# Second batch's product with x in three fp32r products of 512 columns, turned back through DRAM

## The chip, the cores and the metric

One core of one Trainium2 chip. The time is that of the whole program on the device, in microseconds (us), the median of the runs shown. Engines: PE (TensorE) multiplies, DVE (VectorE), ACT (ScalarE) and POOL (GpSimd) do the rest, SP (SyncE) issues most DMAs.

## What is computed

x is (8, 512, 128): 8 batches of 512 tokens, in float32. Per batch:

```
xn  = layernorm(layernorm(x)) * gamma + beta
q, k, v = split(xn @ w_qkv); k = softmax over the tokens
attn = (k^T v per head) applied to q * 32**-0.5, @ w_out + b_out
x1  = x + layernorm(attn + y)                 y = layernorm(x)
x1n = layernorm(x1)
ffn = sum over 8 experts of (silu(x1n @ Wg) * (x1n @ Wu)) @ Wd     Wg, Wu (128, 512), Wd (512, 128)
out = x1 + layernorm(ffn)
```

## The kernel before

The feed-forward part is the bulk of it. Each batch has 32 steps (STEPS: 8 experts times 4 blocks of 128 hidden columns), and a body of the program is one batch, b from 0 to 7. A step s does three 512-column products into a gate bank, three into an up bank and, for the step three before it (LAG), three into the accumulator `acc_ps`. Three products stand for one float32 product: operands are split into fp32r parts `_hi` and `_lo`, and `products` (L1248) adds hi*hi, hi*lo and lo*hi. ACT takes silu of the gate bank (L777), DVE multiplies it with the up bank (L1050), ACT copies the result to `h_hi` (L752) and DVE subtracts to get `h_lo` (L1037). Up to step 29 of the first batch (H_IN_PSUM) h is written back into the up bank, of which there are three. So the up product of step s + 3 waits, in `gate_up` (L1255), for `h_lo` of step s (`s_read`, `s_hlo`).

Between these steps the attention part of the next batch is done in small pieces. Which piece runs at which step on which engine is written in tables: FIRST_PE, FIRST_DVE, FIRST_ACT and FIRST_POOL for body 0 (which does the second batch's attention), PE_AT and so on for the others. Every engine runs its own list in order. On ACT and DVE a piece named in FRONT stands ahead of the step's own work, others behind it; on PE a piece stands behind the step's nine products; on POOL pieces stand ahead of the weight blocks of LO_AT. In body 0 the weights are still being loaded and split: SP loads block m into one of six raw buffers, once POOL has made the lo part of block m - 6 (`load_w`, L461 to L472), ACT makes the hi part (HI_AT), POOL the lo part (`split_lo`, L395), block m one step after ACT. Block m is matrix m % 3 (gate, up, down) of expert m // 3; its products start at step 4 * (m // 3).

The attention of a batch is folded. With E = exp(k - max) it makes A from E and the normalised x (piece A), M by the heads (piece M: eight small matmuls in `through_heads`, L1280, for the second batch; two full products with a mask for later ones), G = wq M (piece G), then x times G into `att_ps` (piece attn). For batches from the third on x times G is done with G as the stationary operand, in three fp32r products of 512 columns. That gives the result transposed, so it is turned back: DVE transposes 32x32 blocks into `t_blk["z"]` (piece z_T, L957), SP stores them to a DRAM tensor and loads them in four pieces into `t_out["z"]` (`store_blocks`, `load_blocks`, L496 to L503), and DVE adds `yb` to get z (L965). `t_blk["z"]` is the same buffer as `t_blk["E"]`, and `t_out["z"]` the same as `zn`. For the second batch (body 0, `first`) the product has x as the stationary operand: four float32 products of 128 columns (L1321), which leave tokens on the partitions, and z is one addition out of PSUM (L962). Behind z come its statistics (z_stats), POOL's rstd, zn and x1, DVE's x1_stats, POOL's x1n and again a turn through DRAM (x1n_T) for the next body's gate and up products.

Of the kernel before, what the change touches and what calls it, by code (L numbers as in the profile page):

```python
# [33 lines left out]
FIRST_DVE = {"E_T": 4, "next_stats": 8, "A": 12, "M": 13, "z": 15, "z_stats": 16, "next_T": 18, "wk_lo": 20,  # L34
             "x1_stats": 20, "x1n_T": 24, "next_xnT_lo": 28, "x1n_lo": 31}
FIRST_ACT = {"E_store": 5, "E_load": 8, "G": 14, "wk_hi": 18, "next_xnT": 26, "next_xnT_hi": 27, "x1n_hi": 30}
FIRST_POOL = {"y": 2, "yb": 6, "next_rstd": 10, "next_xn": 13, "z_rstd": 17, "x1": 17, "x1_rstd": 21}
# [47 lines left out]
def build(nc, x, gamma, beta, w_qkv, w_out, b_out, Wg, Wu, Wd, out):  # L85
# [10 lines left out]
    with ctx:  # L96
# [120 lines left out]
        att_v = att_ps[:, :].rearrange("p (j d) -> p j d", j=J)  # L217
# [241 lines left out]
        def _(sp):  # L459
# [26 lines left out]
            for m in range(6, NW):  # L486
                load_w(m)
                if m == 8:
                    sp.wait_ge(s_f_x1ps, J)
                    load_x(2, 0)  # L490

# [8 lines left out]
            def load_blocks(k, n):  # L500
                sp.wait_ge(s_t_store[k], n * 16)
                for dst, src in exchange(k):
                    sp.dma_start(dst, src).then_inc(s_t_load[k], 16)  # L503

            def body(b, par, first, nxt, last):
                if nxt and not first:
                    sp.wait_ge(s_x1, b)
                    load_x(b + 2, par)
                if not first:
                    if not last:  # L510
                        store_blocks("E", s_E_blk, b + 1)
                    store_blocks("acc", s_acc, b)
                    if not last:
                        load_blocks("E", b + 1)
                    load_blocks("acc", b)

                if not first and not last:
                    store_blocks("z", s_z_blk, b)

                    sp.wait_ge(s_x1, b)  # L520
                    load_blocks("z", b)
# [169 lines left out]
        def _(act):  # L691
# [5 lines left out]
            def attention(at, c, par, first):  # L697
# [188 lines left out]
        def _(dve):  # L886
# [24 lines left out]
            def attention(at, c, par, first):  # L911
# [10 lines left out]
                if at == "wk_lo":  # L922
                    dve.wait_ge(s_wk_hi, 1)
                    dve.tensor_tensor(wk_lo[:, :], wqkv[:, D:2 * D], wk_hi[:, :].bitcast(F32),
                                      ALU.subtract).then_inc(s_wk_lo, 1)
                if at == "next_xnT_lo":
                    dve.wait_ge(s_xnT_hi, c - 1)
                    dve.tensor_tensor(xnT_lo[:, :], xnT[:, :], xnT_hi[:, :].bitcast(F32),
                                      ALU.subtract).then_inc(s_xnT_lo, 1)
# [28 lines left out]
                if at == "z":  # L958
                    dve.wait_ge(s_yb, c)
                    if first:  # L960
                        dve.wait_ge(s_attn_ps, c)
                        dve.tensor_tensor(z[:, :, :], att_v, yb[:, :, :], ALU.add).then_inc(s_z, 1)  # L962
                    else:
                        dve.wait_ge(s_t_load["z"], (c - 1) * 64)
                        dve.tensor_tensor(z[:, :, :].rearrange("p j (i r) -> p j i r", r=32), from_group(t_out["z"][:, :]),  # L965
                                          yb[:, :, :].rearrange("p j (i r) -> p j i r", r=32), ALU.add).then_inc(s_z, 1)
# [12 lines left out]
                if at == "E_T":  # L979
                    dve.wait_ge(s_ET, c)  # L980
                    if c > 2:

                        dve.wait_ge(s_t_store["z"], (c - 2) * 16)
# [263 lines left out]
        def _(pe):  # L1247
# [39 lines left out]
            def attention(at, c, first):  # L1287
                if at == "kT":
                    pe.wait_ge(s_xnT_hi, c - 1)
                    products(att_ps[:, :], wk_hi[:, :], wk_lo[:, :], pairs(xnT_hi[:, :]), pairs(xnT_lo[:, :]), True, True,  # L1290
                             s_xnT_lo, c - 1).then_inc(s_kT_ps, 1)
# [20 lines left out]
                if at == "attn" and not first:  # L1312

                    pe.wait_ge(s_G, c)
                    pe.wait_ge(s_G_lo, c - 1)
                    products(att_ps[:, :], G_hi[:, :], G_lo[:, :], pairs(xnT_hi[:, :]), pairs(xnT_lo[:, :]), True, True,
                             s_xnT_lo, c - 1).then_inc(s_attn_ps, 1)
                elif at == "attn":
                    pe.wait_ge(s_G, c)
                    for j in range(J):  # L1320
                        last = pe.matmul(att_ps[:, j * D:j * D + D], xnT[:, j * P:j * P + P], G_sb[:, :],  # L1321
                                         start=True, stop=True)
                    last.then_inc(s_attn_ps, 1)
# [272 lines left out]
```

## Time and profile before

| | |
|---|---|
| median of 3 runs | 542.60 us (542.57 to 542.65) |
| the profiled execution's own time | 542.58 us |
| its span, first to last instruction | 540.7 us |
| mean granted TensorE clock | 0.999 of full speed |
| busy share of the span | PE 99%, weight loads 86%, DVE 82%, ACT 64%, POOL 31% |
| DMA traffic | 28.68 MB, mean 53 GB/s |

The time of a run is a little more than the span, since it holds what lies around the program. Times in the rows are us from the span's start. Matmuls are pipelined: a record's length is longer than the distance to the next start, so the pace of PE is read from start times. Some instructions of a float32 product appear as two records.

### The profile page before, as it was taken

To read this page: it belongs to the slowest core of one execution; us is meant where nothing else is said; L and a number is where in the kernel's file an instruction comes from. 1 tells how busy PE (TensorE), PEld (TensorE's weight loads), DVE (VectorE), ACT (ScalarE), POOL (GpSimd) and SP (SyncE) were. 2 spreads that over 40 slices of the span, in tenths; PEclk is the share of its full clock that TensorE was granted. 3 is DMA by queue.
4 is the path that set the end of the run, shared out by engine and by line. 5 is a ranking of instruction groups with operands and counts; after the bars stand their busy time and mean duration, and the time that the engine had idled before them with its cause. 6 is when DMAs were issued, how large, how long until landed. Compare 5 with 4: busy or idle time off the path is not lost.

```text
span 540.7 us, 8660 instructions
## 1 busy us (share of the span) xinstructions
PE 534.3 (99%) x2584; PEld 466.2 (86%) x2584; DVE 442.5 (82%) x967; ACT 348.4 (64%) x633; POOL 169.0 (31%) x221
## 2 busy tenths in 40 slices
PE   8999999999999999999999999999999999999997
PEld 6788888888888888888888888888888888888886
DVE  7896877899777997879977898688987799777866
ACT  5986877557674565855667566665767555655555
POOL 6796950217102280114602045021540016000101
PEclk9999999999999999999999999999999999999999
DMA  6354111120220201202102112021111110110000
GB/s 199 108 168 116 41 59 50 30 78 21 60 73 7 96 23 39 79 19 79 52 8 79 40 59 59 0 79 39 60 39 44 35 61 0 41 39 1 20 2 19
DMA packets 33797, 28.68 MB, mean 53 GB/s; under 512 B 3411, under 2 KB 25686, under 8 KB 33750
## 3 DMA queue, kind: packets, MB, share of 16 engines
q1 hardware_dynamic: 32736, 27.47, 16.2%
q10 hardware_dynamic: 1014, 0.66, 0.4%
q8 instruction: 20, 0.33, 0.3%
q14 instruction: 27, 0.22, 0.1%
HBM read 17.37 MB, written 10.75 MB: 52 GB/s over the span
## 4 chain that ended last, share of the span: by engine, by line
PE 98%; ACT 1%; DVE 1%; DMA 0%; issue 0%; POOL 0%; DVEq 0%; POOLq 0%; SPq 0%
PE acc_att_ps L1251 11%; PE acc_att_ps L1250 11%; PE acc_att_ps L1253 11%; PE gate_ps L1250 10%; PE gate_ps L1251 10%; PE up_ps L1251 10%; PE up_ps L1250 10%; PE gate_ps L1253 10%; PE up_ps L1253 10%; PE acc_att_ps L1296 1%; DMA x_in<-in_L_attn_x_dram 0%; ACT xh L843 0%; PE acc_att_ps L1311 0%; PE acc_att_ps L1308 0%; PE acc_att_ps L1302 0%
## 5 line engine op out<-in xcount | busy, mean ns | idle before, releaser
L777 ACT ACTIVATE gs<-gate_ps 128x512 f32<-128x512 f32 x255 | 152.2, 597 | 171.3 <-PE gate_ps L1253 170.3
L1050 DVE TENSOR_TENSOR h<-gs,up_ps 128x512 f32<-128x512 f32 x231 | 157.5, 682 | 75.8 <-PE up_ps L1253 65.9
L1037 DVE TENSOR_TENSOR h_lo<-h,h_hi 128x512 fp32r<-128x512 f32 x230 | 171.5, 745 | 0.0
L752 ACT ACTIVATE h_hi<-h 128x512 fp32r<-128x512 f32 x230 | 143.5, 624 | 6.5 <-DVE h L1050 5.1
L1250 PE MATMUL gate_ps<-x1nT_hi,wg_hi 128*128 128x512 f32 (+1 forms) x254 | 98.4, 387 | 0.0
L1251 PE MATMUL gate_ps<-x1nT_hi,wg_lo 128*128 128x512 f32 (+1 forms) x254 | 96.1, 378 | 0.0
L1253 PE MATMUL gate_ps<-x1nT_lo,wg_hi 128*128 128x512 f32 (+1 forms) x254 | 96.1, 378 | 0.0
L1250 PE MATMUL up_ps<-x1nT_hi,wu_hi 128*128 128x512 f32 (+1 forms) x254 | 96.1, 378 | 0.0
L1251 PE MATMUL up_ps<-x1nT_hi,wu_lo 128*128 128x512 f32 (+1 forms) x254 | 96.1, 378 | 0.0
L1253 PE MATMUL up_ps<-x1nT_lo,wu_hi 128*128 128x512 f32 (+1 forms) x254 | 96.1, 378 | 0.0
L1250 PE MATMUL acc_att_ps<-h_hi,wd_hi 128*128 128x512 f32 x252 | 95.5, 379 | 0.0
L1251 PE MATMUL acc_att_ps<-h_hi,wd_lo 128*128 128x512 f32 x252 | 95.5, 379 | 0.0
L1253 PE MATMUL acc_att_ps<-h_lo,wd_hi 128*128 128x512 f32 x252 | 95.5, 379 | 0.0
L550 POOL TENSOR_TENSOR rstd_fin<-mv_fin,expo 128x4 f32<-128x4 f32 (+2 forms) x10 | 8.8, 888 | 172.2 <-DVE mv_fin L890 140.0
L1253 PEld LDWEIGHTS up_ps<-x1nT_lo,wu_hi 128*128 128x128 f32 x254 | 48.0, 189 | 6.8
L1253 PEld LDWEIGHTS acc_att_ps<-h_lo,wd_hi 128*128 128x128 f32 x252 | 47.6, 189 | 7.2
L1253 PEld LDWEIGHTS gate_ps<-x1nT_lo,wg_hi 128*128 128x128 f32 x254 | 48.0, 189 | 6.8
L1251 PEld LDWEIGHTS up_ps<-x1nT_hi,wu_lo 128*128 128x128 f32 x254 | 48.0, 189 | 6.8
L1250 PEld LDWEIGHTS up_ps<-x1nT_hi,wu_hi 128*128 128x128 f32 x254 | 48.0, 189 | 6.8
L1251 PEld LDWEIGHTS acc_att_ps<-h_hi,wd_lo 128*128 128x128 f32 x252 | 47.6, 189 | 6.7
L1250 PEld LDWEIGHTS acc_att_ps<-h_hi,wd_hi 128*128 128x128 f32 x252 | 47.6, 189 | 6.7
L1251 PEld LDWEIGHTS gate_ps<-x1nT_hi,wg_lo 128*128 128x128 f32 x254 | 48.1, 189 | 6.0
(296 smaller groups left out, 565.0 us busy)
## 6 DMA issues: line engine op xcount, KB each, us to landing
w_raw<-in_L_ffn_Wg_dram SPq DMA_DIRECT2D x8, 256.0 KB, 3.0
w_raw<-in_L_ffn_Wu_dram SPq DMA_DIRECT2D x8, 256.0 KB, 2.9
w_raw<-in_L_ffn_Wd_dram SPq DMA_DIRECT2D x8, 256.0 KB, 2.9
x_in<-in_L_attn_x_dram SPq DMA_DIRECT2D x7, 256.0 KB, 2.9
t_dram_x1n<-t_blk_x1n SPq DMA_DIRECT2D x7, 256.0 KB, 2.0
t_out_x1n<-t_dram_x1n SPq DMA_DIRECT2D x28, 64.0 KB, 1.9
t_dram_acc<-t_blk_acc SPq DMA_DIRECT2D x7, 256.0 KB, 2.3
t_out_acc<-t_dram_acc SPq DMA_DIRECT2D x28, 64.0 KB, 2.0
```

The lines of the kernel that those rows point to most:

```text
L550: pool.tensor_tensor(rstd[k][:, 0, toks], mv[k][:, toks, 1], expo[:, toks], ALU.pow).then_inc(done, 1)
L752: act.activation(h_hi[s % NH][:, :], h_of(t, s)[:, :], ACT.Copy).then_inc(s_hhi, 1)
L777: act.activation(gs[q][:, :], gate_ps[q][:, :], ACT.Silu).then_inc(s_silu, 1)
L1037: dve.tensor_tensor(h_lo[s % NH][:, :], h_of(t, s)[:, :], h_hi[s % NH][:, :].bitcast(F32), ALU.subtract).then_inc(s_hlo, 1)
L1050: dve.tensor_tensor(h_of(t, s)[:, :], gs[q][:, :], up_ps[q][:, :], ALU.mult).then_inc(s_h, 1)
L1250: pe.matmul(ps, w_h, x_h, start=start, stop=False)
L1251: pe.matmul(ps, w_l, x_h, start=False, stop=False)
L1253: return pe.matmul(ps, w_h, x_l, start=False, stop=stop)
L1296: last = pe.matmul(att_ps[:, 0:D].rearrange("p (i r) -> p i r", r=32), xh[:, j, :], from_group(t_out["E"][:, :])[:, j], start=(j == 0), st ...
```

## The change

The second batch's x times G takes the form that the later batches have. PE does three fp32r products of 512 columns. ACT makes G_hi for it as for the others, DVE makes G_lo at step 14. Its x is split too: ACT makes `xnT_hi` at step 10 (own_xnT_hi) and DVE `xnT_lo` at step 11 (own_xnT_lo). Since this batch's `xnT` has its columns in another order, the two write through a view that puts them in the order of the other batches, with a step of two elements. The result is turned back: z_T at step 15, SP's store and four loads, z at step 18 instead of 15, z_stats at 18 instead of 16, next_T at 17 instead of 18, x1_stats at 21 instead of 20. On POOL z_rstd and x1 move from step 17 to 20, x1_rstd from 21 to 22. SP does the store and the loads ahead of the last weight block's load. M for this batch stays with the products through the heads. The counts that later batches wait for go up by one.

```diff
-FIRST_DVE = {"E_T": 4, "next_stats": 8, "A": 12, "M": 13, "z": 15, "z_stats": 16, "next_T": 18, "wk_lo": 20,
-             "x1_stats": 20, "x1n_T": 24, "next_xnT_lo": 28, "x1n_lo": 31}
-FIRST_ACT = {"E_store": 5, "E_load": 8, "G": 14, "wk_hi": 18, "next_xnT": 26, "next_xnT_hi": 27, "x1n_hi": 30}
-FIRST_POOL = {"y": 2, "yb": 6, "next_rstd": 10, "next_xn": 13, "z_rstd": 17, "x1": 17, "x1_rstd": 21}
+FIRST_DVE = {"E_T": 4, "next_stats": 8, "own_xnT_lo": 11, "A": 12, "M": 13, "G": 14, "z_T": 15, "next_T": 17,
+             "z": 18, "z_stats": 18, "wk_lo": 20, "x1_stats": 21, "x1n_T": 24, "next_xnT_lo": 28, "x1n_lo": 31}
+FIRST_ACT = {"E_store": 5, "E_load": 8, "own_xnT_hi": 10, "G": 14, "wk_hi": 18, "next_xnT": 26, "next_xnT_hi": 27,
+             "x1n_hi": 30}
+FIRST_POOL = {"y": 2, "yb": 6, "next_rstd": 10, "next_xn": 13, "z_rstd": 20, "x1": 20, "x1_rstd": 22}
...
+        def in_two_by_two(v):
+            return v.rearrange("p (h l q) -> p h l q", h=JH, l=JH)
+
+        def pairs_of_two_by_two(v):
+            return v.rearrange("p (l q h) -> p h l q", h=JH, l=JH)
...
-            for m in range(6, NW):
+            for m in range(6, NW - 1):
                 load_w(m)
                 if m == 8:
                     sp.wait_ge(s_f_x1ps, J)
                     load_x(2, 0)
...
+            store_blocks("z", s_z_blk, 1)
+            load_blocks("z", 1)
+            load_w(NW - 1)
...
+                if at == "own_xnT_hi":
+                    act.wait_ge(s_xnT, 1)
+                    act.activation(pairs_of_two_by_two(xnT_hi[:, :]), in_two_by_two(xnT[:, :]),
+                                   ACT.Copy).then_inc(s_xnT_hi, 1)
...
+                if at == "own_xnT_lo":
+                    dve.wait_ge(s_xnT_hi, 1)
+                    dve.tensor_tensor(pairs_of_two_by_two(xnT_lo[:, :]), in_two_by_two(xnT[:, :]),
+                                      pairs_of_two_by_two(xnT_hi[:, :]).bitcast(F32), ALU.subtract).then_inc(s_xnT_lo, 1)
...
                 if at == "z":
                     dve.wait_ge(s_yb, c)
-                    if first:
-                        dve.wait_ge(s_attn_ps, c)
-                        dve.tensor_tensor(z[:, :, :], att_v, yb[:, :, :], ALU.add).then_inc(s_z, 1)
-                    else:
-                        dve.wait_ge(s_t_load["z"], (c - 1) * 64)
-                        dve.tensor_tensor(z[:, :, :].rearrange("p j (i r) -> p j i r", r=32), from_group(t_out["z"][:, :]),
-                                          yb[:, :, :].rearrange("p j (i r) -> p j i r", r=32), ALU.add).then_inc(s_z, 1)
+                    dve.wait_ge(s_t_load["z"], c * 64)
+                    dve.tensor_tensor(z[:, :, :].rearrange("p j (i r) -> p j i r", r=32), from_group(t_out["z"][:, :]),
+                                      yb[:, :, :].rearrange("p j (i r) -> p j i r", r=32), ALU.add).then_inc(s_z, 1)
...
-                if at == "attn" and not first:
+                if at == "attn":
 
                     pe.wait_ge(s_G, c)
-                    pe.wait_ge(s_G_lo, c - 1)
+                    pe.wait_ge(s_G_lo, c)
                     products(att_ps[:, :], G_hi[:, :], G_lo[:, :], pairs(xnT_hi[:, :]), pairs(xnT_lo[:, :]), True, True,
-                             s_xnT_lo, c - 1).then_inc(s_attn_ps, 1)
-                elif at == "attn":
-                    pe.wait_ge(s_G, c)
-                    for j in range(J):
-                        last = pe.matmul(att_ps[:, j * D:j * D + D], xnT[:, j * P:j * P + P], G_sb[:, :],
-                                         start=True, stop=True)
-                    last.then_inc(s_attn_ps, 1)
+                             s_xnT_lo, c).then_inc(s_attn_ps, 1)
```

What the tables do to the order is seen at three places. The first is DVE at steps 11 to 13 of body 0, between the step's own pairs of `up_ps` (h, in the up bank) and `h_lo`. Before:

```order
L935 RECIPROCAL erec<-esum 128x1
L939 COPY A_sb<-acc_att_ps 128x128
L1050 TENSOR_TENSOR up_ps<-gs,up_ps 128x512
L1037 TENSOR_TENSOR h_lo<-up_ps,h_hi 128x512
L948 SCALAR_TENSOR_TENSOR M_sb<-acc_att_ps,erec,R_sb 128x128
```

Now:

```order
L942 TENSOR_TENSOR xnT_lo<-xnT,xnT_hi 128x2x256
L953 RECIPROCAL erec<-esum 128x1
L957 COPY A_sb<-acc_att_ps 128x128
L1064 TENSOR_TENSOR up_ps<-gs,up_ps 128x512
L1051 TENSOR_TENSOR h_lo<-up_ps,h_hi 128x512
L966 SCALAR_TENSOR_TENSOR M_sb<-acc_att_ps,erec,R_sb 128x128
```

xnT_lo stands ahead of erec and A_sb, for which PE's products through the heads wait.

The second is DVE from z on, steps 15 to 18. Before:

```order
L962 TENSOR_TENSOR z<-acc_att_ps,yb 128x512
L1050 TENSOR_TENSOR up_ps<-gs,up_ps 128x512
L1037 TENSOR_TENSOR h_lo<-up_ps,h_hi 128x512
L1050 TENSOR_TENSOR up_ps<-gs,up_ps 128x512
L1037 TENSOR_TENSOR h_lo<-up_ps,h_hi 128x512
L904 BN_STATS st_z<-z 128x6 x4
L890 BN_AGGR mv_z<-st_z 128x2 x4
L900 TENSOR_SCALAR nm_z<-mv_z 128x4
L1050 TENSOR_TENSOR up_ps<-gs,up_ps 128x512
L1037 TENSOR_TENSOR h_lo<-up_ps,h_hi 128x512
L1050 TENSOR_TENSOR up_ps<-gs,up_ps 128x512
L1037 TENSOR_TENSOR h_lo<-up_ps,h_hi 128x512
```

Now:

```order
L975 STREAM_TRANSPOSE t_blk_E<-acc_att_ps 128x512
L1064 TENSOR_TENSOR up_ps<-gs,up_ps 128x512
L1051 TENSOR_TENSOR h_lo<-up_ps,h_hi 128x512
L1064 TENSOR_TENSOR up_ps<-gs,up_ps 128x512
L1051 TENSOR_TENSOR h_lo<-up_ps,h_hi 128x512
L1064 TENSOR_TENSOR up_ps<-gs,up_ps 128x512
L1051 TENSOR_TENSOR h_lo<-up_ps,h_hi 128x512
L991 STREAM_TRANSPOSE t_blk_x<-xh 128x512
L979 TENSOR_TENSOR z<-zn,yb 128x512
L1064 TENSOR_TENSOR up_ps<-gs,up_ps 128x512
L1051 TENSOR_TENSOR h_lo<-up_ps,h_hi 128x512
L918 BN_STATS st_z<-z 128x6 x4
```

A transpose into t_blk_E (the shared block buffer) has z's place; z comes three steps later, behind next_T's transpose of x, and ahead of step 18's h; its statistics follow h and h_lo.

The third is SP and POOL. SP before, and now:

```order
L472 DMA w_raw<-in_L_ffn_Wu_dram 128x512
L472 DMA w_raw<-in_L_ffn_Wd_dram 128x4x128
L498 DMA t_dram_x<-t_blk_x 128x512
L503 DMA t_out_x<-t_dram_x 32x4x128 x4
```

```order
L478 DMA w_raw<-in_L_ffn_Wu_dram 128x512
L498 DMA t_dram_z<-t_blk_E 128x512
L503 DMA zn<-t_dram_z 32x4x128 x4
L478 DMA w_raw<-in_L_ffn_Wd_dram 128x4x128
L498 DMA t_dram_x<-t_blk_x 128x512
L503 DMA t_out_x<-t_dram_x 32x4x128 x4
```

POOL before, and now:

```order
L395 TENSOR_TENSOR wd_lo<-w_raw,wd_hi 128x512
L550 TENSOR_TENSOR rstd_z<-mv_z,expo 128x4
L565 TENSOR_SCALAR zn<-z,nm_z,rstd_z 128x128 x4
L598 TENSOR_TENSOR x_1<-zn,x_in 128x512
L395 TENSOR_TENSOR wg_lo<-w_raw,wg_hi 128x512
L395 TENSOR_TENSOR wu_lo<-w_raw,wu_hi 128x512
L395 TENSOR_TENSOR wd_lo<-w_raw,wd_hi 128x512
```

```order
L395 TENSOR_TENSOR wd_lo<-w_raw,wd_hi 128x512
L395 TENSOR_TENSOR wg_lo<-w_raw,wg_hi 128x512
L395 TENSOR_TENSOR wu_lo<-w_raw,wu_hi 128x512
L560 TENSOR_TENSOR rstd_z<-mv_z,expo 128x4
L575 TENSOR_SCALAR zn<-z,nm_z,rstd_z 128x128 x4
L608 TENSOR_TENSOR x_1<-zn,x_in 128x512
L395 TENSOR_TENSOR wd_lo<-w_raw,wd_hi 128x512
```

On SP the turn of z stands between the loads of blocks 22 and 23. On POOL the lo parts of blocks 18 and 19 have moved ahead of rstd_z, zn and x1.

## Rows read from the trace of the kernel before

**Rows 1.** The page's head: span, then busy time of each engine.
```profile
span 540.7 us, 8660 instructions
...
PE 534.3 (99%) x2584; PEld 466.2 (86%) x2584; DVE 442.5 (82%) x967; ACT 348.4 (64%) x633; POOL 169.0 (31%) x221
```

**Rows 2.** The chain that ended last, share of the span by engine.
```profile
PE 98%; ACT 1%; DVE 1%; DMA 0%; issue 0%; POOL 0%; DVEq 0%; POOLq 0%; SPq 0%
```

**Rows 3.** What PE waited for: us in total, times, longest.
```profile
PE up_ps L1407 <- DVE warm L1075: 1.0, 1, 1.0
PE gate_ps L1533 <- ACT x1nT_hi L860: 0.6, 1, 0.6
```

**Rows 4.** PE's timeline in body 0: start, us, engine, line, operation, out<-in, count.
```profile
42.82 0.43 PE L1284 MATMUL acc_att_ps<-U_sb,A_sb 128*32 128x128 f32 x8
...
47.39 1.05 PE L1321 MATMUL acc_att_ps<-G_sb,xnT 128*128 128x128 f32 x8
48.20 0.46 PE L1250 MATMUL gate_ps<-x1nT_hi,wg_hi 128*128 128x512 f32 x1
48.50 0.38 PE L1251 MATMUL gate_ps<-x1nT_hi,wg_lo 128*128 128x512 f32 x1
...
60.59 0.38 PE L1250 MATMUL up_ps<-x1nT_hi,wu_hi 128*128 128x512 f32 x1
```

**Rows 5.** PE's timeline in body 1, the third batch's product with x.
```profile
108.77 0.38 PE L1250 MATMUL acc_att_ps<-xnT_hi,G_hi 128*128 128x512 f32 x1
...
109.42 0.38 PE L1250 MATMUL gate_ps<-x1nT_hi,wg_hi 128*128 128x512 f32 x1
109.63 0.38 PE L1251 MATMUL gate_ps<-x1nT_hi,wg_lo 128*128 128x512 f32 x1
```

**Rows 6.** DVE's timeline in body 0.
```profile
31.90 1.17 DVE L1037 TENSOR_TENSOR h_lo<-h,h_hi 128x512 fp32r<-128x512 f32 x1
...
40.98 0.29 DVE L939 COPY A_sb<-acc_att_ps 128x128 f32<-128x128 f32 x1
...
51.76 0.70 DVE L1050 TENSOR_TENSOR up_ps<-gs,up_ps 128x512 f32<-128x512 f32 x1 [0.65 <-PE up_ps L1253]
...
52.96 0.86 DVE L904 BATCH_NORM_STATS2 st_z<-z 128x6 f32<-128x128 f32 x4
...
54.48 0.70 DVE L1050 TENSOR_TENSOR up_ps<-gs,up_ps 128x512 f32<-128x512 f32 x1
...
56.88 0.70 DVE L977 STREAM_TRANSPOSE t_blk_x<-xh 128x512 f32<-128x512 f32 x1
```

**Rows 7.** POOL's timeline in body 0.
```profile
30.78 1.73 POOL L592 TENSOR_TENSOR yb<-y,bout_bc 128x512 f32<-128x512 f32 x1
...
40.47 1.27 POOL L395 TENSOR_TENSOR wg_lo<-w_raw,wg_hi 128x512 fp32r<-128x512 f32 x1
...
54.34 1.01 POOL L550 TENSOR_TENSOR rstd_z<-mv_z,expo 128x4 f32<-128x4 f32 x1 [2.26 <-DVE mv_z L890]
...
58.52 1.28 POOL L395 TENSOR_TENSOR wg_lo<-w_raw,wg_hi 128x512 fp32r<-128x512 f32 x1
```

**Rows 8.** DMA issues in SP's timeline: start, time of issuing, queue, line, out<-in, count.
```profile
49.28 0.33 SPq L472 DMA_DIRECT2D w_raw<-in_L_ffn_Wu_dram  x1
...
112.46 2.85 SPq L503 DMA_DIRECT2D zn<-t_dram_z  x4
...
175.38 0.34 SPq L498 DMA_DIRECT2D t_dram_z<-t_blk_E  x1
177.45 1.73 SPq L503 DMA_DIRECT2D zn<-t_dram_z  x4
...
435.45 0.34 SPq L498 DMA_DIRECT2D t_dram_z<-t_blk_E  x1
438.71 1.77 SPq L503 DMA_DIRECT2D zn<-t_dram_z  x4
```

**Rows 9.** DMA issues by kind: count, KB each, median us from issue to landing.
```profile
zn<-t_dram_z SPq DMA_DIRECT2D x24, 64.0 KB, 1.9
```

More of the change, by code:

```diff
@@ L216, in build @@
         att_ps = two_ps[:, 512:1024]
-        att_v = att_ps[:, :].rearrange("p (j d) -> p j d", j=J)
         z_ps = [ps[:, 0:D] for ps in (gate_ps[1], up_ps[1], gate_ps[2], acc_ps)]
@@ L485, in _ @@
             sp.dma_start(bout_bc[:, :], b_out.rearrange("(a d) -> a d", a=1).to_broadcast([P, D])).then_inc(s_bout, 16)
-            for m in range(6, NW):
[L487 to L490, printed above, removed]
             def store(c):
@@ L503, in load_blocks @@
                     sp.dma_start(dst, src).then_inc(s_t_load[k], 16)
+            for m in range(6, NW - 1):
+                load_w(m)
+                if m == 8:
+                    sp.wait_ge(s_f_x1ps, J)
+                    load_x(2, 0)
+            store_blocks("z", s_z_blk, 1)
+            load_blocks("z", 1)
+            load_w(NW - 1)
             def body(b, par, first, nxt, last):
@@ L517, in body @@
                 if not first and not last:
-                    store_blocks("z", s_z_blk, b)
+                    store_blocks("z", s_z_blk, b + 1)
                     sp.wait_ge(s_x1, b)
-                    load_blocks("z", b)
+                    load_blocks("z", b + 1)
                 if nxt:
@@ L731, in attention @@
                     act.wait_ge(s_G_ps, c)
-                    act.activation(G_sb[:, :] if first else G_hi[:, :], att_ps[:, 0:D], ACT.Copy).then_inc(s_G, 1)
+                    act.activation(G_hi[:, :], att_ps[:, 0:D], ACT.Copy).then_inc(s_G, 1)
                 if at == "x1n_hi":
@@ L925, in attention @@
                                       ALU.subtract).then_inc(s_wk_lo, 1)
+                if at == "own_xnT_lo":
+                    dve.wait_ge(s_xnT_hi, 1)
+                    dve.tensor_tensor(pairs_of_two_by_two(xnT_lo[:, :]), in_two_by_two(xnT[:, :]),
+                                      pairs_of_two_by_two(xnT_hi[:, :]).bitcast(F32), ALU.subtract).then_inc(s_xnT_lo, 1)
                 if at == "next_xnT_lo":
-                    dve.wait_ge(s_xnT_hi, c - 1)
+                    dve.wait_ge(s_xnT_hi, c)
                     dve.tensor_tensor(xnT_lo[:, :], xnT[:, :], xnT_hi[:, :].bitcast(F32),
@@ L980, in attention @@
                     dve.wait_ge(s_ET, c)
-                    if c > 2:
-                        dve.wait_ge(s_t_store["z"], (c - 2) * 16)
+                    if c > 1:
+                        dve.wait_ge(s_t_store["z"], (c - 1) * 16)
                     dve.transpose(grouped(t_blk["E"][:, :]), by_group(ET[:, :])).then_inc(s_E_blk, 1)
@@ L1288, in attention @@
                 if at == "kT":
-                    pe.wait_ge(s_xnT_hi, c - 1)
+                    pe.wait_ge(s_xnT_hi, c)
                     products(att_ps[:, :], wk_hi[:, :], wk_lo[:, :], pairs(xnT_hi[:, :]), pairs(xnT_lo[:, :]), True, True,
-                             s_xnT_lo, c - 1).then_inc(s_kT_ps, 1)
+                             s_xnT_lo, c).then_inc(s_kT_ps, 1)
                 if at == "A":
```

## The prediction

> **What bounds the kernel now.** I read the page's head first: PE is busy in 99% of a span of 540.7 us [rows 1]. Busy time alone doesn't make a bound, so the chain that ended last comes next: 98% of it is PE [rows 2]. The list of what PE waited for settles it: five waits, 2.5 us in sum, all of one occurrence, and the last in time is that on x1nT_hi ahead of the very first gate product (L1533); the longest two stand in [rows 3]. From there on PE never waits. So two things count: PE time added or removed behind that goes into the span one to one, and work on any other engine costs nothing until a product stands waiting for it. A 512-column product starts 0.21 to 0.22 us after the one before it [rows 5]; a step of nine takes 1.94 us.
>
> **The edit on PE.** Before, the four 128-column float32 products L1321 run as eight records from 47.39 us, the next gate product starts at 48.20 and the one behind it at 48.50 [rows 4]: 1.11 us from the first record to the gate's second product. In the third batch the same place already has three fp32r products of 512 columns: 108.77 to 109.42, and 109.63 for the gate's second product, 0.86 us [rows 5]. The difference, 0.25 us, contains both the products and the slower start of the gate product behind them. It is the only PE work that changes: **-0.25 us**, and everything on PE behind step 14 comes that much earlier. Eight records for four products say that float32 takes more than one pass. The Trainium skill (TensorE: Matmul & The Clock Gate, section "Wait — 56ns, not 53.3ns?") gives 55.6 ns start to start for 128 columns at the high clock and 215.7 ns for 512; by that alone the old form would be 0.44 us, the new one 0.65, and the edit would cost 0.20 us instead of gaining 0.25.
>
> **The split of xnT.** ACT's copy to xnT_hi stands behind h_hi at step 10. ACT is busy in 64% of the span [rows 1], so one more copy, even one stretched to over 1 us by its 8-byte step, is caught up within a step or two. Price 0. The DVE subtraction xnT_lo comes behind h_lo at step 11 and ahead of erec and A_sb (40.98 us before), on which PE's products through the heads wait. It reads two SBUF tiles, and POOL runs wg_lo from 40.47 for 1.27 us, so POOL is there first [rows 6, 7]. At 31.90 such a subtraction took 1.17 us instead of 0.68: it ended 0.56 us behind the end of POOL's yb [rows 6, 7]. So xnT_lo ends about 42.3, and A_sb (0.29 us [rows 6]) about 42.6 where it ended at 41.3; PE's products start at 42.82 [rows 4]. Price 0, with 0.1 to 0.2 us to spare. Bounds: nothing, and 1.1 us if POOL's next operation (1.3 us) goes ahead as well; I take 0, since at 31.90 DVE got its turn behind one POOL operation. G_lo reads 128 columns as A_sb does, 0.3 us, behind G_hi on ACT; G's products are a step of 1.94 us ahead of those that need it at 47.39, and DVE waits for PE in each of these steps: 0.
>
> **The way back through DRAM.** Before, z was one addition out of PSUM, done right behind the product. Now: a transpose (0.70 us, as [rows 6] show for t_blk_x) that ends near 49.0; the store by SP; four loads; z at step 18. SP reaches the store behind load_w of block 22, which waits for POOL's wu_lo and went out at 49.28 [rows 8]. So the store goes out about 49.65. In a typical later batch the first load follows 2.07 us behind the store (175.38, 177.45), the four are issued in 1.73 us [rows 8] and each lands 1.9 us after its issue [rows 9]: last landing 49.65 + 2.07 + 1.30 + 1.9 = **54.9 us**. In the last batch the first load came 3.26 us behind the store (435.45, 438.71) and in the third batch the four issues took 2.85 us [rows 8]: these late ones put the landing at 56.1, both together (with loads that then land later) at about 57.3.
>
> DVE itself gets to z no earlier: without z's statistics at step 16, step 17's h goes out when PE is ready for it, 53.45 (step 16's was at 51.76 [rows 6]; a step of 1.94 later, 0.25 earlier), then h_lo and t_blk_x, so z is reached at 55.35. There it meets POOL again, because wg_lo of block 18, held behind zn and x1 before (58.52, [rows 7]), now runs as soon as ACT has made wg_hi, which ACT does at the end of step 17: an estimate of 54.4 to 55.65, 0.95 us behind that step's h and 1.27 long. By the 31.90 row DVE is free about 0.5 us behind that end: h of step 18 at 56.15. Then h_lo of 17 (57.35), the statistics (1.52 us, 52.96 to 54.48 [rows 6]), h of 19 at 58.87, h_lo of 18 done at 60.15. Who waits for that: PE's up product of step 21 overwrites the PSUM bank h_lo reads; it started at 60.59 [rows 4], now 60.34. **Margin 0.2 us**, price 0.
>
> The second limit: rstd_z starts 1.38 us behind the start of z's statistics (52.96, 54.34) and x1 is ready 4.18 us later (58.52) [rows 6, 7]: now 58.73 and 62.9, perhaps 63.2 with wk_lo colliding with zn. DVE's x1 statistics at step 21 therefore start at 63.2, h of 22 at 64.7, h_lo of 21 is done at 66.0; the up product of step 24 wants it at 66.17. Again 0.2 us. Behind that all is loose: x1n is ready about 67.4, DVE turns it at 68.3 anyway; POOL's three last lo blocks end near 71, PE wants them from 73.3; load_w of block 23 goes out behind the z loads, near 53.8, and ACT converts it at step 23, over 10 us later; t_blk_x's store goes out earlier than before.
>
> **Sum.** 542.58 (the profiled execution, span 540.7 and what lies around it) - 0.25 + 0 = 542.33. The median of the runs shown is 542.60, 0.02 above; I predict **542.35 us**. A measurement of this kernel tells from no change about 0.2%, 1.1 us; my forecast is inside it.
>
> **Rivals.**
> 1. The z round trip is late and PE pays. Each 0.1 us that the data land behind about 55.7 us comes off the 0.2 us margin and then stalls PE as much. One late piece (56.1): stall 0.4 to 0.6, total 542.7. For it: load_w's 256 KB go ahead of the store on the same queue, and the tightest margins are 0.2 us, while my landing times are good to 0.5. Against: four of six later round trips took the typical time and leave 0.7 us.
> 2. The same place, both pieces late (57.0 and more): DVE stands at z, behind it h of 18, h_lo of 17 and 18, and PE at step 21 for 1.4 us or more: 543.7 to 544.0, slower by over 0.2%. It decides from a landing at 57.0 on. For it: each of the two delays shows in one of the six round trips of the trace. Against: never both in one.
> 3. PE waits at the products through the heads. If POOL's wu_lo goes ahead of xnT_lo too, A_sb is ready near 43.8 and PE loses 1.0 us: 543.3. The order in which DVE and POOL take turns decides. In the rows DVE waited for one operation only. The Trainium skill (SBUF — State Buffer, section "SBUF: two separate sides") has it that whichever of the two starts first holds the shared port pair for its whole instruction and the other is blocked fully; the 1.17 us row agrees for one instruction, and the page doesn't say who is next.
> 4. The new products are not cheaper. If the old form cost only what 128-column products cost at one pass each, the time is about 542.8. The start times of 47.39 and 48.20 speak against it, since PE is full on both sides. The page's rates above would bring this.
> 5. It does more than its 0.25 us on PE: nothing in the list of PE's waits is left to remove, so faster by over 1.1 us has no mechanism here.
>
> **How the numbers follow.** Forecast 0.62 (542.2 to 542.5); rival 1 0.22 (542.5 to 543.2); rival 2 0.06; rival 3 0.06 (543.0 to 543.6); rival 4 0.02; rival 5 0.02. The range 542.2 to 543.2 holds the forecast, rival 1 and part of rivals 3 and 4, 0.87 in all, and leaves out little more than rival 2. Within 0.2% are the forecast, rivals 1 and 4 and nearly all of 3: 0.91; slower 0.07; faster 0.02.
>
> **What would show it.** Right: three records of acc_att_ps from xnT_hi and xnT_lo at 47.4 us, 0.65 us to the gate product; the list of PE's waits with the same five rows; xnT_lo lasting about 1.5 us with A_sb ending before 42.8; z starting near 55.4 and lasting 0.8 us; h_lo of step 18 done before 60.3. Wrong: a new row in PE's waits on h_lo (rivals 1, 2) or on A_sb (rival 3), or DVE idle ahead of z until a DMA. A time below 541.5 would mean that the old products cost more than their start times say.

## The result and the profile after

| | before | after |
|---|---|---|
| median | 542.60 us (542.49 to 542.81, 5 runs) | 544.55 us (544.42 to 544.62, 5 runs) |
| span of the profiled execution | 540.7 us | 542.8 us |
| mean granted TensorE clock | 0.999 | 0.999 |
| ratio after / before | | 1.0035, 95% interval 1.0024 to 1.0046 |

The change costs 1.9 to 2.1 us. The forecast of 542.35 and its range up to 543.2 are both missed, on the side of rival 2. Runs of one kernel spread by about 0.7 us (the kernel before in a later series: 542.39 to 543.12), so amounts below that are read from start times within the traces.

The page's head of the kernel after, beside [rows 1]; PE's busy time is longer by 0.8 us only, so most of the 2.1 us must be idle time.

```profile
span 542.8 us, 8662 instructions
...
PE 535.1 (99%) x2579; PEld 466.1 (86%) x2579; DVE 445.5 (82%) x970; ACT 349.0 (64%) x634; POOL 169.5 (31%) x221
```

What PE waited for, the first three rows. Beside [rows 3] there is one new row, and it is now the largest: up products that wait for `h_lo`.

```profile
PE up_ps L1264 <- DVE h_lo L1051: 1.5, 2, 1.0
PE up_ps L1415 <- DVE warm L1089: 1.0, 1, 1.0
PE gate_ps L1541 <- ACT x1nT_hi L874: 0.6, 1, 0.6
```

PE's timeline, beside [rows 4, 5]: the new product at 47.46, the two waits, and the third batch's product, the place of [rows 5].

```profile
47.46 0.38 PE L1264 MATMUL acc_att_ps<-xnT_hi,G_hi 128*128 128x512 f32 x1
...
48.10 0.38 PE L1264 MATMUL gate_ps<-x1nT_hi,wg_hi 128*128 128x512 f32 x1
48.32 0.38 PE L1265 MATMUL gate_ps<-x1nT_hi,wg_lo 128*128 128x512 f32 x1
...
58.25 0.38 PE L1267 MATMUL gate_ps<-x1nT_lo,wg_hi 128*128 128x512 f32 x1
59.63 0.45 PE L1264 MATMUL up_ps<-x1nT_hi,wu_hi 128*128 128x512 f32 x1 [1.00 <-DVE h_lo L1051]
59.92 0.38 PE L1265 MATMUL up_ps<-x1nT_hi,wu_lo 128*128 128x512 f32 x1
...
61.43 0.38 PE L1267 MATMUL gate_ps<-x1nT_lo,wg_hi 128*128 128x512 f32 x1
62.26 0.48 PE L1264 MATMUL up_ps<-x1nT_hi,wu_hi 128*128 128x512 f32 x1 [0.45 <-DVE h_lo L1051]
62.58 0.38 PE L1265 MATMUL up_ps<-x1nT_hi,wu_lo 128*128 128x512 f32 x1
...
110.55 0.38 PE L1264 MATMUL acc_att_ps<-xnT_hi,G_hi 128*128 128x512 f32 x1
```

From 47.46 to 48.32 are 0.86 us where 1.11 stood: the product gains its 0.25 us. Then the up product of step 20 starts 1.38 us behind the gate product instead of 0.22 (1.16 lost), and the one behind it 0.29 later instead of 0.22 (0.07). At step 21 it is 0.83 (0.61 lost) and 0.32 (0.10). In sum 1.94 us are lost at two instructions. Body 0 also ran 0.07 us later from the start (42.89 for the products through the heads, which did not wait, against 42.82). 1.94 + 0.07 - 0.25 = 1.76, and at the third batch's product the kernel is 110.55 - 108.77 = 1.78 us late. The rest, 0.3 us, comes at 290 us, in body 4, where the change touches nothing:

```profile
290.01 0.38 PE L1265 MATMUL acc_att_ps<-h_hi,wd_lo 128*128 128x512 f32 x1
290.42 0.48 PE L1267 MATMUL acc_att_ps<-h_lo,wd_hi 128*128 128x512 f32 x1
290.74 0.38 PE L1264 MATMUL gate_ps<-x1nT_hi,wg_hi 128*128 128x512 f32 x1
```

0.41 and 0.32 us stand where 0.22 and 0.22 are usual. The list of waits doesn't count this gap.

Why `h_lo` is late stands in the timelines of SP, DVE and POOL of body 0, to be read beside [rows 8], [rows 6] and [rows 7].

```profile
49.34 0.33 SPq L478 DMA_DIRECT2D w_raw<-in_L_ffn_Wu_dram  x1
49.71 0.43 SPq L498 DMA_DIRECT2D t_dram_z<-t_blk_E  x1
53.27 1.75 SPq L503 DMA_DIRECT2D zn<-t_dram_z  x4
```

```profile
40.76 1.74 DVE L942 TENSOR_TENSOR xnT_lo<-xnT,xnT_hi 128x512 fp32r<-128x512 f32 x1
42.41 0.15 DVE L953 RECIPROCAL erec<-esum 128x1 f32<-128x1 f32 x1
42.49 0.27 DVE L957 COPY A_sb<-acc_att_ps 128x128 f32<-128x128 f32 x1
...
54.73 0.70 DVE L991 STREAM_TRANSPOSE t_blk_x<-xh 128x512 f32<-128x512 f32 x1
56.84 1.44 DVE L979 TENSOR_TENSOR z<-zn,yb 128x512 f32<-128x512 f32 x1 [1.41 <-DMA zn<-t_dram_z]
58.21 0.68 DVE L1064 TENSOR_TENSOR up_ps<-gs,up_ps 128x512 f32<-128x512 f32 x1
58.80 0.68 DVE L1051 TENSOR_TENSOR h_lo<-up_ps,h_hi 128x512 fp32r<-128x512 f32 x1
59.41 0.86 DVE L918 BATCH_NORM_STATS2 st_z<-z 128x6 f32<-128x128 f32 x4
...
60.91 0.70 DVE L1064 TENSOR_TENSOR up_ps<-gs,up_ps 128x512 f32<-128x512 f32 x1
61.52 0.68 DVE L1051 TENSOR_TENSOR h_lo<-up_ps,h_hi 128x512 fp32r<-128x512 f32 x1
```

```profile
54.52 1.28 POOL L395 TENSOR_TENSOR wg_lo<-w_raw,wg_hi 128x512 fp32r<-128x512 f32 x1 [2.60 <-ACT wg_hi L705]
56.46 1.28 POOL L395 TENSOR_TENSOR wu_lo<-w_raw,wu_hi 128x512 fp32r<-128x512 f32 x1 [0.66 <-ACT wu_hi L705]
```

The chain that ended last runs through the same places; its rows for the store and for the last of the four loads (start, length, what it was):

```profile
49.71 3.54 DMA t_dram_z<-t_blk_E
...
54.59 2.16 DMA zn<-t_dram_z
```

The store goes out at 49.71 and the first load only 3.56 us behind it. DVE has done t_blk_x at 55.43 and stands at z for 1.41 us. When the data are there, at 56.8, POOL has been in wu_lo of block 19 since 56.46, and z takes 1.44 us instead of about 0.68. `h` of step 18 and `h_lo` of step 17 stand behind z on DVE: they free the bank that PE wants at step 20. Then the statistics of z stand between that h_lo and the next, so PE waits again at step 21.

### The profile page after: what moved, and what is told of

The parts are those of the page before. It is cut to its first block, busy times and chain, and to the rows that moved or that the text cites. A ratio compares the mean times of both kernels' runs of the same rounds, so it can differ in the third digit from the quotient of the medians.

```text
span 542.8 us, 8662 instructions
## 1 busy us (share of the span) xinstructions
PE 535.1 (99%) x2579; PEld 466.1 (86%) x2579; DVE 445.5 (82%) x970; ACT 349.0 (64%) x634; POOL 169.5 (31%) x221
## 4 chain that ended last, share of the span: by engine, by line
PE 95%; DMA 1%; DVE 1%; ACT 1%; issue 1%; SPq 0%; POOL 0%; DVEq 0%; ACTq 0%
PE acc_att_ps L1267 10%; PE acc_att_ps L1264 10%; PE acc_att_ps L1265 10%; PE up_ps L1264 10%; PE gate_ps L1264 10%; PE gate_ps L1267 10%; PE up_ps L1267 10%; PE gate_ps L1265 10%; PE up_ps L1265 10%; PE acc_att_ps L1310 1%; PE up_ps L1415 1%; DMA t_dram_z<-t_blk_E 1%; DMA zn<-t_dram_z 0%; ACT xh L857 0%; PE acc_att_ps L1325 0%
```

## Experiments

The theory: the store of 256 KB is in flight together with load_w of block 22, another 256 KB, issued 0.37 us ahead of it; that makes it 1.5 us longer than one alone, and everything else follows from z's place on DVE. The load of block 21 overlaps the store as well: SP issued it at 47.88, 1.83 us ahead of the store, and it landed 2.9 us behind its issue. Its rivals: the order on SP's queue alone delays it; or POOL's lo part of block 19 is the cost; or the split of x, the new product or the changed order costs time by themselves. The e and f kernels up to f4 are the changed kernel with one edit each, apart from f1 and f2, which with g1 and g2 are about another question and are told last. They ran in three series (e, f, g); the kernel before had medians of 542.70, 542.61 and 542.61 us in them, each of 21 runs or more, and every ratio is against the runs of its own series.

**e1: turn ahead of load 22.**

```
-            for m in range(6, NW - 1):
+            for m in range(6, NW - 2):
...
             load_blocks("z", 1)
+            load_w(NW - 2)
             load_w(NW - 1)
```

> The changed kernel, with SP's store and loads of z moved ahead of the load of block 22 as well, so that no weight load is in flight beside the store; all else as in the changed kernel. Theory Q (a store issued right behind a 256 KB load lands 1.5 us later, and that is the cause of the loss): the store goes out at 49.1 us, the first load of z 2.0 to 2.1 us later instead of 3.56, z's data are there near 54.4 before DVE asks at 55.4, z waits for POOL's lo part of block 18 at most, PE waits for no h_lo, and the time is 542.3 to 542.5 us. Rival S (the store is slow in this place whatever stands ahead of it, for the first use of the DRAM tensor or the DMA engines' state): 3.3 to 3.6 us between store and first load again, z at 56.2, the time 543.8 or more. Rival D (the new order of DVE and POOL costs PE by itself): short round trip, but PE still waits for h_lo by 0.5 us or more in sum.

Measured: 542.69 us (542.45 to 543.14), ratio 1.0001 (0.9992 to 1.001), span 541.0. No PE wait on h_lo. SP and z:

```profile
47.96 0.33 SPq L478 DMA_DIRECT2D w_raw<-in_L_ffn_Wg_dram  x1
49.13 0.33 SPq L498 DMA_DIRECT2D t_dram_z<-t_blk_E  x1
51.86 1.75 SPq L503 DMA_DIRECT2D zn<-t_dram_z  x4
...
55.44 1.00 DVE L980 TENSOR_TENSOR z<-zn,yb 128x512 f32<-128x512 f32 x1
```

With one line moved on SP the 1.9 us are gone. The time is 0.2 us above what was expected, since the 0.3 us in body 4 are still there. The store still overlaps load 21, issued 1.17 us ahead, and takes 2.73 us to the first load.

**e2: the store by ACT's queue.** SP's `store_blocks("z", ...)` is taken out, and ACT does it in its step 15.

```
+                if at == "z_store":
+                    act.wait_ge(s_z_blk, 1)
+                    act.dma_start(t_dram["z"][:, :], t_blk["z"][:, :]).then_inc(s_t_store["z"], 16)
```

> The changed kernel, with z's store issued by ACT's queue at the end of step 15 (about 50.0 us) instead of SP's at 49.7; the loads of z stay on SP behind the load of block 22. If the 256 KB load delays the store because both stand in one queue (theory Q1), the store lands 2.0 us after its issue, the first load of z goes out near 52.1, z starts near 55.4, and the time is 542.3 to 542.6 us. If the two share the DMA engines or the memory whatever queue they come from (theory Q2), the store takes 3 us or more again, the first load goes out at 53.0 or later, and the time is 543.8 to 544.8 us. Rival S expects what Q2 does.

Measured: 544.63 us (543.73 to 545.04), ratio 1.0035 (1.0022 to 1.0047), span 543.2; PE waits 1.4 us for h_lo at two places, as in the change. The store's issue on ACT, and SP:

```profile
49.49 0.34 ACTq L741 DMA_DIRECT2D t_dram_z<-t_blk_E  x1
```

```profile
48.33 0.33 SPq L478 DMA_DIRECT2D w_raw<-in_L_ffn_Wg_dram  x1
49.77 0.33 SPq L478 DMA_DIRECT2D w_raw<-in_L_ffn_Wu_dram  x1
53.66 1.76 SPq L503 DMA_DIRECT2D zn<-t_dram_z  x4
```

4.17 us from store to first load, though the store now goes out ahead of load 22 and on another queue: one load was issued 1.16 us ahead of it and one 0.28 us behind, and the latter took 4.0 us itself. So the place in SP's queue is not the cause: transfers of two queues slow each other. That they share what moves them is what the Trainium skill says (DMA: Bandwidth & Descriptors, section "Issuing engines are not separate DMA queues"): transfers from different engines run on the same 16 DMA engines and interleave. This trace agrees with it by 4.17 us beside 2.02 for a store almost alone (f4 below).

**e3: POOL's lo part of block 19 one step later.**

```
-LO_AT = {5: 1, 6: 3, **{m: when + 1 for m, when in HI_AT.items()}}
+LO_AT = {5: 1, 6: 3, **{m: when + (1 if m != 19 else 2) for m, when in HI_AT.items()}}
```

> The changed kernel, with POOL's lo part of block 19 moved from step 19 to step 20, behind z_rstd, zn and x1, so that POOL is idle when z's data land at 56.8 us. In the changed kernel z took 1.44 us there instead of 0.65. Theory L (POOL's operation held DVE's z back by 0.75 us, which went into PE's waits one to one): z takes 0.65 us, PE's two waits for h_lo shrink from 1.5 us in sum by 0.7 to 0.8, the time is 543.7 to 543.9 us. Rival (z's length is its own, from its strided operands, or PE's wait is set by something else): z takes 1.4 us again and the time stays within 0.2 us of 544.55.

Measured: 544.51 us (544.41 to 544.64), ratio 1.0034 (1.0021 to 1.0046): nothing gained. z is short now, yet PE waits at three places:

```profile
56.76 0.69 DVE L979 TENSOR_TENSOR z<-zn,yb 128x512 f32<-128x512 f32 x1 [1.51 <-DMA zn<-t_dram_z]
...
65.53 1.12 DVE L914 TENSOR_SCALAR nm_x<-mv_x 128x4 f32<-128x4 f32 x1
```

```profile
58.79 0.45 PE L1264 MATMUL up_ps<-x1nT_hi,wu_hi 128*128 128x512 f32 x1 [0.35 <-DVE h_lo L1051]
...
61.42 0.48 PE L1264 MATMUL up_ps<-x1nT_hi,wu_hi 128*128 128x512 f32 x1 [0.45 <-DVE h_lo L1051]
...
68.00 0.45 PE L1264 MATMUL up_ps<-x1nT_hi,wu_hi 128*128 128x512 f32 x1 [0.48 <-DVE h_lo L1051]
```

z is 0.75 us shorter and the first wait shrinks from 1.00 to 0.35 us, with data that came 0.1 us later by PE's steps; so POOL's part in it was 0.65 to 0.75 us. The expected 543.7 to 543.9 us did not come, for POOL's two lo blocks now run at 64.11 and 65.36, over the statistics of x1, where nm_x takes 1.12 us instead of 0.17 and makes h_lo of step 21 late. POOL's part in the loss is real, but moving its work by one step only moved the collision.

**e4: the new product, without the way through DRAM.** z is added out of PSUM at step 18 (`dve.tensor_tensor(z[:, :, :], att_v, yb[:, :, :], ALU.add)` behind `s_attn_ps`), and z_T, the store and the loads of this batch are taken out. The kernel leaves out the transposition of the second batch's product; all other work and its order are that of the change.

> The changed kernel without the turn through DRAM for the second batch: no transpose, no store, no loads of z; z is added straight out of PSUM at step 18, so that part of the computation (the transposition of the second batch's attention result) is left out. The product in three fp32r products, the splits of xnT and the later places of z, its statistics and x1 all stay. If only the round trip costs, PE's time is what the product saves and no wait for h_lo is in the list: 542.3 to 542.4 us. If the later places of z, statistics and POOL's work alone cost PE time (rival D), PE waits for h_lo by 0.3 us or more and the time is 542.7 or more.

Measured: 542.36 us (542.17 to 542.79), ratio 0.9994 (0.9986 to 1.0003), span 540.4. No PE wait on h_lo, no gap in body 4. So the product, the splits and the moved steps together give what the forecast said of them; the whole loss is in the turn.

**f3: the late data as they are, z one step later.**

```
-             "z": 18, "z_stats": 18, "wk_lo": 20, "x1_stats": 21, "x1n_T": 24, "next_xnT_lo": 28, "x1n_lo": 31}
+             "z": 19, "z_stats": 19, "wk_lo": 20, "x1_stats": 22, "x1n_T": 25, "next_xnT_lo": 28, "x1n_lo": 31}
...
-FIRST_POOL = {"y": 2, "yb": 6, "next_rstd": 10, "next_xn": 13, "z_rstd": 20, "x1": 20, "x1_rstd": 22}
+FIRST_POOL = {"y": 2, "yb": 6, "next_rstd": 10, "next_xn": 13, "z_rstd": 21, "x1": 21, "x1_rstd": 23}
```

> The changed kernel with SP's order left alone (store behind the load of block 22, landing late), and what follows the turn one step later: z and z_stats at step 19, POOL's z_rstd and x1 at 21, x1_stats at 22, x1_rstd at 23, x1n_T at 25. Theory Q (the data are late, and DVE standing at z with h of step 18 behind it passes that to PE): the round trip still takes 3.5 us or more and the data still land at 56.8, but h of step 18 is ahead of z in the queue; PE's waits for h_lo fall from 1.5 us to 0 to 0.2, the time is 542.5 to 542.9 us (with the 0.3 us gap in body 4). Rival D (the load of z, statistics and splits on DVE and POOL is what PE waits for, wherever z stands): PE's waits stay at 0.7 us or more, the time is above 543.4.

Measured: 542.72 us (542.45 to 543.01), ratio 1.0 (0.9991 to 1.0008), span 540.8; no PE wait on h_lo.

```profile
49.64 0.43 SPq L498 DMA_DIRECT2D t_dram_z<-t_blk_E  x1
53.43 1.75 SPq L503 DMA_DIRECT2D zn<-t_dram_z  x4
...
55.39 0.70 DVE L1064 TENSOR_TENSOR up_ps<-gs,up_ps 128x512 f32<-128x512 f32 x1
56.00 0.68 DVE L1051 TENSOR_TENSOR h_lo<-up_ps,h_hi 128x512 fp32r<-128x512 f32 x1
56.82 1.39 DVE L979 TENSOR_TENSOR z<-zn,yb 128x512 f32<-128x512 f32 x1
```

The data are as late as in the change (3.79 us behind the store) and POOL is in the way as before (z takes 1.39 us), and it costs nothing: h of step 18 and h_lo of 17 have gone ahead. A late transfer has a price only for what is queued behind the instruction that waits for it.

**f4: the turn ahead of loads 21, 22 and 23.** As e1, with `range(6, NW - 3)` and the three loads behind the turn.

> The changed kernel with z's turn ahead of the loads of blocks 21, 22 and 23, so that no weight load has been issued for about 2.4 us when the store goes out. A dose of the same cause: from store to first load 4.17 us with one load 1.2 us ahead and one 0.3 us behind it, 3.56 with one 0.37 us ahead, 2.73 with one 1.17 us ahead. Theory Q2 (loads and store share the DMA engines or the memory, whatever the queue): 2.0 to 2.1 us here, no wait of PE for h_lo, and the time that of e1, 542.6 to 542.75. Rival S (the place or the first use of the DRAM tensor adds to it): 2.5 us or more.

Measured: 542.73 us (542.54 to 543.29), ratio 1.0002 (0.9993 to 1.0011), span 540.8.

```profile
46.65 0.38 SPq L478 DMA_DIRECT2D w_raw<-in_L_ffn_Wd_dram  x1
49.01 0.33 SPq L498 DMA_DIRECT2D t_dram_z<-t_blk_E  x1
51.03 1.75 SPq L503 DMA_DIRECT2D zn<-t_dram_z  x4
```

2.02 us from store to first load where the last 256 KB load went out 2.36 us ahead and landed 2.7 us after its issue, 0.3 us into the store. So neither the place in the program nor the first use of the DRAM tensor delays the store. With the other traces this is a row of doses of the disputed term: 2.02 (one load about to land), 2.55 to 2.73 (one load, 1.1 to 1.2 us ahead: e1, and f2 and g1 below), 3.56 to 3.84 (two, 0.37 and 1.8 us ahead: the change, f3, e3), 4.17 (two around it: e2). The distance of the nearest load may not set it alone: x's store in this same trace, 1.64 us behind the last of three loads issued one after the other, took 3.42 us, though a packet of the kind described next was in flight beside it.

Late stores occur without a load beside them too. In the trace before, 3 of 15 turns with a single store took 2.84 to 3.26 us from store to first load instead of 2.0 to 2.1, at 329.75, 394.76 and 435.45. All twelve traces are late at the first of these places (2.8 to 3.4) and at the last (2.4 to 4.4). A packet of one of the two queues that the profile calls `instruction` was in flight in each of these three (at 330.1, 396.5 and 435.8); that it is the cause is not shown, and another such packet, at 479.5 us, stood in a turn of 2.04. Beside z's store in body 0 there is none in any of the eight traces that have this store; in the change the nearest stand at 40 and 58.5 us. So this second way to be late has no part in the loss.

**The 0.3 us in body 4.** Like the change, e1, e2, e3, f3 and f4 have a gap of 0.41 or 0.42 us between 288 and 291 us, in the same place of the program; before and e4 have none. Ahead of it DVE starts h 0.35 us later behind ACT's silu than usual (1.61 us of idle time, 1.26 before at 286.95). DVE's timeline of the change:

```profile
286.76 0.71 DVE L998 STREAM_TRANSPOSE t_blk_E<-ET 128x512 f32<-128x512 f32 x1 [0.65 <-ACT ET L733]
289.08 0.69 DVE L1064 TENSOR_TENSOR h<-gs,up_ps 128x512 f32<-128x512 f32 x1 [1.61 <-ACT gs L791]
```

Four kernels asked whether it hangs on where DVE's program stands, by its count of instructions. Each adds one-column memsets to a tile that nothing reads:

```
+            for i in range(n):
+                dve.memset(spare[:, i:i + 1], 0.0)
```

f1 is the kernel before with three at the start of DVE's program:

> The kernel before, with three more instructions on DVE at its start (memsets of one column of a spare tile). In the changed kernel and in the variants with the turn, which have three DVE instructions more than before, PE has a gap of 0.41 us instead of 0.21 ahead of an h_lo product in body 4 (near 288 us), because a DVE multiplication started 0.35 us after its silu had ended; a packet of the instruction queue lies beside it. Theory F (the gap hangs on where in DVE's instruction stream a fetch falls, and not on what the change computes): the same gap appears here near 288 us, and the time is 0.2 to 0.3 us above before. Rival: without the change's work there is no gap, and the time is that of before within 0.05 us.

Measured: 542.59 us (542.39 to 543.06), ratio 1.0 (0.9991 to 1.0008), no gap in body 4. f2 is e1 with eight at the start:

> The variant with the turn ahead of both loads (e1_turn_before_loads, 542.69 us), with eight more one-column memsets on DVE at its start. Theory F: the gap near 288 us is gone, or has moved to a place where DVE has slack, and the time is 542.3 to 542.45 us, 0.2 to 0.35 under e1 and below before by the product's 0.25. Rival: the gap stays at the same product, time 542.7.

Measured: 542.81 us (542.66 to 543.32), ratio 1.0005 (0.9996 to 1.0014). The gap of 0.41 us is gone, but there is a smaller one in its stead (read with g1 below), and the start of the program is 0.7 us longer (a product of step 11 at 40.54 instead of 39.83 us), so no time is won. g1 is e1 with the eight behind step 23 of body 0:

> The first of the runs above, with the turn of z ahead of both last loads, and eight one-column memsets on DVE behind step 23 of the first batch, where DVE has slack, not at the start. Theory F (what costs 0.3 us in body 4, a gap of 0.41 us at 288.6 ahead of the gate product, depends on where DVE's program stands by count of instructions): the gap is gone and, with no later start, the time is 542.4, span 540.7, ahead of the kernel with the turn alone by 0.3. Rival F2 (f2 lost its gap because its start moved 0.7 us, by timing and not by place): the gap stays, 542.7, span 541.0.

Measured: 542.81 us (542.31 to 542.92), ratio 0.9999 (0.9991 to 1.0008), span 541.0 with a granted clock of 0.998 in that execution. The gap of 0.41 us is gone, with the start at 40.03 us, and the 542.4 us expected did not come. g2 is the kernel before with three at that place:

> The kernel before with three one-column memsets on DVE behind step 23 of the first batch, so that DVE's program is as much longer as in the change. Theory F: since three at the start brought no gap, but the turn's own instructions stand in body 0, a gap of 0.41 us near 288.6 and 542.9. Rival F2: no gap, 542.6, span 540.7.

Measured: 542.59 us (542.43 to 543.13), ratio 1.0001 (0.9992 to 1.001), no gap in body 4.

Three more instructions did not bring the gap, at either place; eight took it away at both. But it did not go: it moved. In g1, and likewise in f2 (at 283.41), the h of the step ahead starts 0.35 us late instead. g1's row, and the same instruction in the kernel before:

```profile
282.95 0.69 DVE L1069 TENSOR_TENSOR h<-gs,up_ps 128x512 f32<-128x512 f32 x1 [0.99 <-PE up_ps L1272]
```

```profile
282.43 0.69 DVE L1050 TENSOR_TENSOR h<-gs,up_ps 128x512 f32<-128x512 f32 x1 [0.64 <-PE up_ps L1253]
```

There it costs PE 0.12 us (in f2; 0.13 in g1) instead of 0.30. f1 and g2 have such a late h as well, at 523.73 and 523.80, which the kernel before has not, and it costs PE nothing. And 0.5 to 0.7 us behind each late start looked at stands a packet of the profile's queue `q14 instruction`: at 289.7 for the one at 289.08, at 283.6, 284.0 and 524.3 in g1, f2 and f1. Before has one at 289.0 and e4 at 287.7, without a loss on PE. So the theory that the place goes with DVE's program by count is borne out in part: eight instructions more, at either place, moved the late start to an earlier instruction, the same one in both. The rival, the start's timing, fails: e2 started at 40.16 us and had the gap in its old place, g1 at 40.03 and had not. How many instructions lie between two such places was not counted, and that the packet causes the late start is argued from its place only.

The table has, for each trace, the time from one and the same product of step 11 (39.67 us before) to the last product of h_lo with wd_hi (534.87 us before), which leaves the start-up's scatter out, and its distance to the kernel before (495.20 us).

| kernel | step 11 to the end, us | against before | what is in it |
|---|---|---|---|
| before plus 3 (f1, g2) | 495.19, 495.19 | -0.01 | nothing |
| e4, no turn | 494.94 | -0.26 | the product's gain alone |
| e1, f4, f3 | 495.27, 495.26, 495.34 | +0.06 to +0.14 | gain and the gap |
| g1, f2 | 495.13, 495.08 | -0.07, -0.12 | gain and the smaller gap at 284 us |
| after, e2, e3 | 497.21, 497.21, 497.28 | +2.01 to +2.08 | gain, gap, waits on h_lo |

No version beats the kernel before by what a measurement can tell; e4 comes nearest, and it leaves work out.

## Why the prediction was wrong

**The edit on PE: right.** -0.25 us forecast, 0.86 instead of 1.11 us found, -0.26 in e4. The rate of one pass that the prediction quotes from the Trainium skill (TensorE: Matmul & The Clock Gate), by which it would have been +0.20, is ruled out by the same rows. Rival 4 was priced wrongly: 0.44 us is one pass for each of the eight records; one pass for each of the four products would be 0.22 us by the same rate, an estimate, and 543.0 us instead of 542.8.

**The split of xnT: right.** xnT_lo was locked out by one POOL operation, not two: 1.74 us instead of the 1.5 named, erec behind it at 42.41, and A_sb done at 42.76 before PE came, at 42.89. It was POOL's next operation, wu_lo at 41.75, that was held up in turn (1.90 us instead of 1.29), and with it POOL's later blocks and SP's loads of blocks 19 to 21, by 0.6 us. PE didn't wait for them, but block 21's load went out at 47.88 us instead of about 47.3 and so overlapped z's store by 1.1 us instead of 0.5. The prediction did not look for this; what it added to the store's time no run separates. Rival 3 did not come.

**The way back through DRAM: wrong, and this is the step that failed.** The sum had "last landing 49.65 + 2.07 + 1.30 + 1.9 = 54.9 us"; it was 49.71 + 3.56 + 1.32 + 2.16 = 56.75. The term at fault is the 2.07, taken from a typical later batch, in which SP issues nothing else near the store. The program put the store 0.37 us behind a 256 KB load, and [rows 8] showed that very load at 49.28. The text names it, as a reason for rival 1, but gives it no price in the sum; the runs give it: nothing in f4, +0.7 us in e1, +1.5 in the change, +2.1 in e2, by how much of the loads is in flight.

**What followed from it on DVE.** Planned: z at 55.35, h of step 18 at 56.15. Measured: z at 56.84 (1.49 later), h at 58.21 (2.06 later). The second 0.57 is POOL's lo part of block 19. The plan had POOL's lo part of block 18 in z's way, and its price was in the 56.15; it did not ask which POOL operation a later z would meet. The Trainium skill (SBUF — State Buffer, section "SBUF: two separate sides") has it that whoever starts first holds the shared port pair for the whole instruction; z, started 0.38 us behind wu_lo, ended 0.54 us behind its end, which agrees, and e3 shows the 0.69 us of a z that meets nobody.

**The margins: right.** The plan had h_lo of step 17 done at 57.35; the up product of step 20, which it doesn't name, was then due at 58.40 (58.64 in the trace before, less 0.25), a margin of 1.05 us: 2.06 less 1.05 is the 1.00 us in the row at 59.63. It had h_lo of 18 done 0.19 us ahead of step 21's up product. The trace says 62.20 instead of 60.15, 2.05 later, less 0.19: 1.86 us in sum, and 1.16 + 0.07 + 0.61 = 1.84 were lost up to there. So the model of the queue was good to 0.1 us and was fed with a landing 1.85 us early.

**The rivals.** Rival 2's cost is what came, at 0.06: DVE stood at z and PE at step 21, but PE stood longer at step 20. Only one of its two pieces was late, the first load; the four issues took the usual 1.75 us. By rival 1's rule (each 0.1 us behind 55.7, less a margin of 0.2) the landing at 56.75 gives a stall of 0.85 us, and 1.94 were lost: the rule left out step 20 and POOL. Rival 2 was priced at 543.7 to 544.0 and was to decide from a landing at 57.0; it came at 56.75, since POOL's lock put 0.57 us on top, and the 0.3 us in body 4 lift 544.2 to 544.5. Its chance was worked out as two independent accidents of later round trips (3.26 us in one, 2.85 in another). The delay in the change was no accident: it was written in SP's order. Nor was the 3.26 us one, which recurs at its place in all twelve traces. The second limit, x1's statistics, was 0.2 us away on paper. e3 bears it out roughly: 0.95 us more on nm_x put the up product of step 24 0.64 us late, so some 0.3 us were to spare. The rest of the way (x1n, blocks 21 to 23, the turn of x) was loose as forecast: x's first load came 3.58 us behind its store (2.01 before), with load_w of block 23 issued 0.48 us ahead of it, and nothing waited for it.

## What to carry to other kernels

A transfer's time from another place of the program holds only with the same neighbours in flight: list every transfer issued within some 2 to 3 us on every queue, and price the overlap, before subtracting a margin from it. Where DVE or any engine with an order of its own has to wait for a DMA, put the wait behind what others wait for, one step later; here that alone was worth 1.8 us with data that were just as late. Issuing the store ahead of the loads (e1, f4) was worth as much. And when something slips by a microsecond, ask again what it meets: the second engine's lock was free of cost at the planned time and cost 0.6 us at the real one.

## What the runs showed of the hardware

- A store of 256 KB to DRAM and loads of 256 KB slow each other, on one queue and across two: 2.0 us from store to first load alone, 2.55 to 2.73 us with one load issued 1.1 to 1.2 us ahead, 3.56 to 4.17 with two beside it; the second of these loads took 3.3 to 4.0 us itself, where it took 2.8 in e4, without the store.
- A small operation of DVE with one input tile was held up as well: nm_x, 128x4, started 0.17 us behind POOL's wd_lo in e3, took 1.12 us instead of 0.17 and ended with it.
- ACT's copy to xnT_hi with an 8-byte step took 0.91 us (at 38.09 in the change) where the copies of the weights, of the same size and without the step, take 0.63; it delayed nobody.
- A start of DVE 0.35 us later than usual, some 230 us behind the change, moved to another instruction when instructions were added elsewhere in DVE's program, and cost PE 0.30, 0.12 or nothing by where it fell. A packet of the queue `q14 instruction` followed each one looked at by 0.5 to 0.7 us; whether that is the cause was not tested.
